# Reciprocal root of a variance: two ScalarE activations and one Newton step in place of a bit trick with longer refinement

## The chip, the core and the metric

The kernel runs on one core of a Trainium2 chip. A core has five engines with an instruction queue each, which run in order and meet only at semaphores: TensorE (PE in the profile), VectorE (DVE), ScalarE (ACT), GpSimd (POOL) and SyncE (SP, which only issues transfers here). The metric is the device time of one execution in microseconds (us), the median of several runs. Lower is better.

## What is computed

Eight blocks (the batch), each of 4096 positions with 32 channels, pass through a linear-attention layer and then through a mixture of 8 experts. Three normalisations over the 32 channels of a position lie on the way; each needs one over the square root of a variance for each position:

```python
def _ln_c(v, eps=1e-06):                       # LN1, input of the attention
    m = jnp.mean(v, axis=1, keepdims=True)
    s = jnp.var(v, axis=1, keepdims=True)
    return (v - m) / jnp.sqrt(s + eps)
...
out = (out - mean) * jax.lax.rsqrt(var + LN_EPS) * g_ln[None, :, None, None]   # LN2, end of the attention
...
def _ln_t(v, eps=1e-05):                       # LN3, input of router and experts
    return (v - m) / jnp.sqrt(s + eps)
x = x + _L0_conv_ref(_ln_c(x), ...)
t = t + _L0_ffn_ref(_ln_t(t), ...)
```

The attention takes a softmax of queries and keys; the second part picks the two best of eight experts for each position and adds their outputs with gates.

## The kernel before

**Tiling.** A block is held as 128 partitions by 32 groups of positions, so that a statistic of a normalisation is a tile of 128x32 numbers (`vsum`, `vari`, `root`, `rr`, `ru`, `rstd`, one of each for LN1, LN2 and LN3), while the data is 128x1024.

**Order.** The order on each engine is written out by hand. The function `iteration(i, cur, prev, nxt, ahead)` goes through 26 steps, and tables with names AT_... say which unit of work stands in which step. An iteration works on four blocks at once: the last part (experts) of block i-1 (`prev`), the attention, LN2 and LN3 of block i (`cur`), the keys and queries of block i+1 (`nxt`), and the load and LN1 of block i+2 (`ahead`). It runs for i = -2 to 8: at -2 only `ahead`, at -1 `nxt` and `ahead`, at 0 all but `prev`, from 1 to 5 all four, at 6 no `ahead`, at 7 only `cur` and `prev`, at 8 only `prev`.

**One normalisation.** DVE sums (`mean`), POOL subtracts the mean (`centered`, L417), ACT squares (`squares`, L486), DVE sums the squares (`vsum`, L653) and then makes the reciprocal root in `inverse_root` (L647): `vari` (L656), a first guess from the bits of the number (`root`, L658), and seven further small steps up to `rstd` (L661 to L679). Each of them waits for the one before. Then POOL multiplies by `rstd` (L422 for LN1 and LN3, L463 for LN2). For LN1 and LN3 ACT then rounds the result twice into `parts` (`high_parts`, L495 and L496), DVE makes the remainder (`low_part`, L684), and TensorE turns the `parts` around through `narrow` (`make_stack`, L842), from where ACT copies them (L490).

**Where the three stand.** LN2: `AT_RSTD2` = steps 10, 11, 11, 12. LN3: `AT_RSTD3` = 19, 19, 20, 20. LN1: `AT_RSTD1` = 22, 23, 23, 24, with LN3's `low_part` (step 22) between the sum and `vari`.

**The turn of an iteration.** TensorE writes `query_logits` of units 0 and 1 (step 0) into the two slots of `narrow`; ACT takes the exponential of each (`query_exp`, tile `eq`, L510), which frees the slot; only then can `make_stack` of LN3's data (step 1) write there. On ACT the two `high_parts` of LN3 (step 22) stand just ahead of these exponentials. On DVE stand at that place: the end of LN3, `sums_ctx` (L733), `grec` (L736), `mix` (L738), `mixz` (L742), `vsum` of LN1, `low_part` of LN3, and the whole root of LN1. TensorE's small product between `sums_ctx` and `grec` is `mix_context` (step 22). `ws_kmax` (L727, step 12) is the DVE addition before which no key logits can be made.

**Tables.** ACT's functions read a table set that an ACT_TABLE_LOAD brings in; before, there is one, ahead of the first copy.

Of the kernel before, what the change touches and what calls it, by code (L numbers as in the profile page):

```python
# [33 lines left out]
P = 128  # L34
G = N // P
# [19 lines left out]
AT_X2 = 13  # L55
AT_CENTER3 = 15
AT_SCALE3 = 21
AT_RSTD2 = (10, 11, 11, 12)
AT_MEAN3 = 15
AT_SQUARE3 = 18  # L60
AT_RSTD3 = (19, 19, 20, 20)
AT_SPLIT3 = 22

AT_STACK3 = (1, 1, 2, 3)
# [9 lines left out]
AT_MEAN1 = 20  # L74
AT_CENTER1 = 20
AT_SQUARE1 = 21
AT_RSTD1 = (22, 23, 23, 24)

AT_SCALE1 = 2
AT_SPLIT1 = 3  # L80
# [16 lines left out]
def build(nc, x, w_qkv, b_qkv, w_out, b_out, g_ln, router_w, router_b, expert_w, expert_b, out):  # L97
# [6 lines left out]
    with ctx:  # L104
# [54 lines left out]
        vsum = {k: sb(f"vsum{k}", [P, G]) for k in LN}  # L159
        vari = {k: sb(f"vari{k}", [P, G]) for k in LN}  # L160
        root = {k: sb(f"root{k}", [P, G]) for k in LN}
        rr = {k: sb(f"rr{k}", [P, G]) for k in LN}
        ru = {k: sb(f"ru{k}", [P, G]) for k in LN}
        rstd = {k: sb(f"rstd{k}", [P, G]) for k in LN}
# [60 lines left out]
        center_ready = {k: sem(f"center_ready{k}") for k in LN}  # L225
        square_ready = {k: sem(f"square_ready{k}") for k in LN}
        rstd_ready = {k: sem(f"rstd_ready{k}") for k in LN}
        xhat_ready = {k: sem(f"xhat_ready{k}") for k in (1, 3)}
        high_ready = {k: sem(f"high_ready{k}") for k in (1, 3)}
        parts_ready = {k: sem(f"parts_ready{k}") for k in (1, 3)}  # L230
# [13 lines left out]
        norm_v = sem("normalise_vector_steps")  # L244
        ln23_v, route_v = sem("layernorm23_vector_steps"), sem("route_vector_steps")
        heads_p, ln2_p, gates_p = sem("heads_pool_steps"), sem("layernorm2_pool_steps"), sem("gates_pool_steps")
        LN1_V, KQ_V, LN23_V, ROUTE_V = 10, 5, 19, 14

        class Chain:

# [227 lines left out]

        @block.scalar
        def _(act):  # L480
            def set_up():
                act.wait_ge(setup_v, SETUP_V)

            def square(k, b):
                act.wait_ge(center_ready[k], 4 * b + 4 if k == 2 else b + 1)
                nc.scalar.activation(squares[k][:], centered[k][:], ACT.Square).then_inc(square_ready[k], 1)  # L486

            def copy_stack(k, pos, u):
                act.wait_ge(narrow_full, pos.n + pos.stack[k][u] + 1)
# [29 lines left out]
            def iteration(i, cur, prev, nxt, ahead):  # L519
                f, g, n, m, pos = i, i - 1, i + 1, i + 2, Places(i, cur, prev, nxt, ahead)  # L520
                for step in STEPS:
                    for u in units(ahead, AT_XT, step):
                        act.wait_ge(narrow_full, pos.n + pos.xt[u] + 1)
                        if cur and u == 0:
                            act.wait_ge(x2_ready, f + 1)
                        nc.scalar.copy(x_tok[:, m % 2, 512 * u:512 * u + 512],
                                       narrow[:, pos.xt[u] % 2, :]).then_inc(narrow_free, 1)
                    for u in units(prev, AT_STACK3, step):
                        copy_stack(3, pos, u)
                    for u in units(cur, AT_QEXP, step):  # L530
                        query_exp(pos, f, u)
                    if ahead and step == AT_SQUARE1:
                        square(1, m)
                    if prev and step == AT_ROUTER:
                        act.wait_ge(small_full, pos.s + pos.logit + 1)
                        nc.scalar.copy(logit[:].rearrange("p g e -> p (g e)"),
                                       small[:, 0:G * E]).then_inc(small_free, 1)
                    if prev and step == AT_RESIDUAL:
                        act.wait_ge(x2_ready, g + 1)
                        if not (isinstance(g, int) and g == 0):  # L540
                            act.wait_ge(out_full, OUTU * g)
                        nc.scalar.copy(residual[:], x2[:]).then_inc(residual_ready, 1)
                    if prev and step == AT_E2:
                        act.wait_ge(gap_ready, g + 1)
                        nc.scalar.activation(e2[:], gap[:], ACT.Exp, scale=wscale[:, 2:3]).then_inc(e2_ready, 1)
                    if nxt and step == AT_SPLIT1:
                        high_parts(1, n, xhat[:, :, 0:C])
                    for u in units(nxt, AT_STACK1, step):
                        copy_stack(1, pos, u)
                    if cur and step == AT_SQUARE2:  # L550
                        square(2, f)
                    if cur and step == AT_SQUARE3:
                        square(3, f)
                    for u in units(nxt, AT_KEXP, step):
                        key_exp(pos, n, u)
                    for half in units(nxt, AT_QROWS, step):
                        act.wait_ge(narrow_full, pos.n + pos.qrows[half] + 1)
                        nc.scalar.copy(qmax_tr[:, half, :],
                                       narrow[:, pos.qrows[half] % 2, 0:P // 2].bitcast(f16)).then_inc(narrow_free, 1)
                    if prev and step in AT_OUT[3::4]:  # L560
                        copy_output(g, AT_OUT.index(step) // 4)
                    if cur and step == AT_SPLIT3:
                        high_parts(3, f, xhat3[:])
# [5 lines left out]
        def _(dve):  # L569
# [77 lines left out]
            def inverse_root(k, c, b, eps, part):  # L647
# [6 lines left out]
                elif part == 1:  # L654
                    c.wait()
                    c.inc(nc.vector.tensor_scalar(vari[k][:], vsum[k][:], 1.0 / C, eps, ALU.mult, ALU.add))  # L656
                    c.wait()
                    c.inc(nc.vector.tensor_scalar(root[k][:].bitcast(i32), vari[k][:].bitcast(i32), -0.5,  # L658
                                                  float(0x5F1FFFF9), ALU.mult, ALU.add))
                    c.wait()  # L660
                    c.inc(nc.vector.tensor_tensor(rr[k][:], root[k][:], root[k][:], ALU.mult))  # L661
                elif part == 2:
                    c.wait()
                    c.inc(nc.vector.scalar_tensor_tensor(ru[k][:], rr[k][:], -0.375 * 0.703952253, vari[k][:],
                                                         ALU.mult, ALU.mult))
                    c.wait()
                    c.inc(nc.vector.scalar_tensor_tensor(root[k][:], ru[k][:], 0.375 * 0.703952253 * 2.38924456,
                                                         root[k][:], ALU.add, ALU.mult))
                    c.wait()
                    c.inc(nc.vector.tensor_tensor(rr[k][:], root[k][:], root[k][:], ALU.mult))  # L670
                else:
                    c.wait()
                    c.inc(nc.vector.scalar_tensor_tensor(ru[k][:], rr[k][:], 64.0 / 9.0, vari[k][:],
                                                         ALU.mult, ALU.mult))
                    c.wait()
                    c.inc(nc.vector.scalar_tensor_tensor(rr[k][:], ru[k][:], -10.0 / 3.0, ru[k][:],
                                                         ALU.add, ALU.mult))
                    c.wait()
                    nc.vector.scalar_tensor_tensor(rstd[k][:], rr[k][:], 5.0, root[k][:], ALU.add,  # L679
                                                   ALU.mult).then_inc(rstd_ready[k], 1)  # L680

            def low_part(k, b, src):
# [358 lines left out]
```

## Time and profile of the kernel before

| | us |
|---|---|
| median of 3 runs | 584.05 (583.22 to 585.13) |
| the profiled execution | 585.64 |
| its span in the trace | 583.9 |

| engine | busy us | share of the span |
|---|---|---|
| PE | 413.1 | 71% |
| DVE | 412.1 | 71% |
| ACT | 236.5 | 41% |
| POOL | 218.9 | 37% |

No engine is busy throughout. So the table alone doesn't say what bounds the kernel; for that one reads the chain that ended last (each piece of work followed back to what released it) and, at a place of interest, the timelines of all engines side by side. In a row of a timeline the first number is the start in us from the start of the span, the second the busy time, and the bracket at the end, where there is one, the idle time before it and what ended it.

### The profile page before, as it was taken

What the parts mean: (1) busy time and instruction counts of PE and PEld (TensorE: products, weight loads), DVE (VectorE), ACT (ScalarE), POOL (GpSimd) and SP (SyncE); (2) the same over time, 40 slices, a digit from 0 to 9 for tenths busy, and PEclk for the clock granted to TensorE, in tenths of its full rate; (3) what the DMA queues carried; (4) which work ended last, traced back from release to release, by engine and by line L of the source; (5) the groups of instructions that cost most, each with busy time, mean ns of one, the idle gap of its engine ahead of it and who ended that gap; (6) DMA issues with size and microseconds to landing.
All of it is one profiled execution on the core that took longest, in us unless ns stands there. A gap on an engine that the chain in (4) does not pass through costs nothing.

```text
span 583.9 us, 9061 instructions
## 1 busy us (share of the span) xinstructions
PE 413.1 (71%) x3632; PEld 329.4 (56%) x3632; DVE 412.1 (71%) x803; ACT 236.5 (41%) x321; POOL 218.9 (37%) x192
## 2 busy tenths in 40 slices
PE   1149968767978497948985797949795898365371
PEld 1027746655767286827764486828682776254261
DVE  0655788599768987598759975898769863864540
ACT  1044635660467035731475046712582137103200
POOL 8200663372336342552237223634255221741100
PEclk9998989795989699877989697959988898885586
DMA  2100000000011000100010001100000001000001
GB/s 50 36 1 1 37 1 12 26 1 2 1 31 43 1 1 12 63 1 1 2 43 30 1 1 35 40 0 1 12 27 2 1 0 38 0 2 16 20 1 36
DMA packets 4257, 9.17 MB, mean 16 GB/s; under 512 B 2134, under 2 KB 2168, under 8 KB 4216
## 3 DMA queue, kind: packets, MB, share of 16 engines
q1 hardware_dynamic: 4216, 8.59, 4.8%
q8 instruction: 29, 0.48, 0.3%
q14 instruction: 12, 0.10, 0.1%
HBM read 4.40 MB, written 4.19 MB: 15 GB/s over the span
## 4 chain that ended last, share of the span: by engine, by line
PE 41%; DVE 36%; ACT 8%; issue 7%; POOL 5%; DMA 2%; POOLq 0%; PEldq 0%; DVEq 0%; ACTq 0%
PE wide L839 12%; PE sums L842 10%; PE small L839 8%; PE narrow L839 7%; DVE gated L785 5%; PE narrow L842 5%; DVE heads L705 5%; DVE kmax L713 4%; ACT stack L490 3%; POOL xhat L422 3%; DVE parts L684 2%; DVE vsum L653 2%; DVE tie L755 2%; DMA x_in<-in_x_dram 2%; DVE zrec L703 2%
## 5 line engine op out<-in xcount | busy, mean ns | idle before, releaser
L785 DVE TENSOR_TENSOR gated<-wide,gates 128x1024 f32<-128x1024 f32 x64 | 77.5, 1222 | 39.4 <-PE wide L839 36.1
L842 PE MATMUL sums<-ident,gated 128*128 128x128 f32 x512 | 79.4, 306 | 34.5 <-DVE gated L785 32.0
L502 ACT ACTIVATE ek<-narrow,wscale 128x512 f32<-128x512 f32 x64 | 44.0, 687 | 142.7 <-PE narrow L839 142.7
L842 PEld LDWEIGHTS sums<-ident,gated 128*128 128x128 f32 x512 | 65.5, 160 | 43.2 <-DVE gated L785 40.2
L839 PE MATMUL wide<-mixz,eq 128*128 128x132 f32 x512 | 73.5, 291 | 5.7 <-ACT stack L490 3.7
L490 ACT COPY stack<-narrow 128x1024 f16<-128x1024 f16 x64 | 63.0, 1014 | 35.1 <-PE narrow L842 35.1
L839 PE MATMUL wide<-w_stack,stack 128*128 128x128 f16 (+1 forms) x512 | 68.5, 280 | 6.9 <-DVE nqmax L690 2.7
L839 PEld LDWEIGHTS wide<-mixz,eq 128*128 128x128 f32 x512 | 65.0, 197 | 6.9 <-ACT stack L490 3.8
L839 PE MATMUL small<-ek,xhat 128*33 128x128 f32 x512 | 67.3, 278 | 0.0
L842 PE MATMUL narrow<-ident,parts 128*128 128x128 f16 x512 | 45.3, 250 | 28.9 <-ACT eq L510 18.9
L439 POOL TENSOR_TENSOR pairs<-heads 128x512 f32<-128x512 f32 x32 | 41.4, 1293 | 56.3 <-DVE heads L705 56.3
L842 PEld LDWEIGHTS narrow<-ident,parts 128*128 128x128 f16 x512 | 39.7, 114 | 33.8 <-DVE parts L684 23.7
L839 PEld LDWEIGHTS small<-ek,xhat 128*33 128x33 f32 x512 | 51.9, 111 | 9.1 <-issue 4.7
L839 PEld LDWEIGHTS wide<-w_stack,stack 128*128 128x128 f16 x512 | 44.3, 109 | 22.2 <-DVE kmax L713 10.0
L839 PE MATMUL wide<-stack,w_stack 128*128 128x512 f16 x64 | 25.1, 487 | 44.0 <-DVE kmax L713 33.3
L422 POOL TENSOR_TENSOR xhat<-centered,rstd 128x1024 f32<-128x1024 f32 x16 | 30.6, 1911 | 62.4 <-DVE rstd L679 62.4
L703 DVE RECIPROCAL zrec<-wide 128x16 f32<-128x16 f32 x64 | 16.4, 256 | 44.8 <-PE wide L839 44.1
L705 DVE TENSOR_TENSOR heads<-wide,zrec 128x512 f32<-128x512 f32 x64 | 44.3, 692 | 2.2
L510 ACT ACTIVATE eq<-narrow,wscale 128x512 f32<-128x512 f32 x64 | 43.1, 689 | 5.5 <-PE narrow L839 5.1
L690 DVE TENSOR_REDUCE nqmax<-wide 128x32 f32<-128x1024 f32 x32 | 39.0, 1219 | 8.6 <-PE wide L839 8.4
L417 POOL TENSOR_TENSOR centered<-x_tok,nmean 128x1024 f32<-128x1024 f32 x8 | 15.3, 1910 | 78.3 <-DVE nmean L645 78.3
L713 DVE TENSOR_REDUCE kmax<-wide 128x1 f32<-128x1024 f32 x32 | 38.1, 1220 | 5.2 <-PE wide L839 4.6
(138 smaller groups left out, 652.8 us busy)
## 6 DMA issues: line engine op xcount, KB each, us to landing
x_in<-in_x_dram SPq DMA_DIRECT2D x8, 512.0 KB
out_dram<-y_out SPq DMA_DIRECT2D x8, 512.0 KB
w_rows<-in_L_ffn_expert_w_dram SPq DMA_DIRECT2D x3, 32.0 KB
w_nat<-in_L_conv_w_qkv_dram SPq DMA_DIRECT2D x1, 48.0 KB
w_rows<-in_L_ffn_router_w_dram SPq DMA_DIRECT2D x3, 1.0 KB
w_rows<-in_L_ffn_expert_b_dram SPq DMA_DIRECT2D x2, 1.0 KB
w_rows<-in_L_ffn_router_b_dram SPq DMA_DIRECT2D x2, 0.0 KB
b_nat<-in_L_conv_b_qkv_dram SPq DMA_DIRECT2D x1, 1.5 KB
```

What stands on the lines that cost most here:

```text
L422: return nc.gpsimd.tensor_tensor(dst, tiles(centered[k][:]), per_tile(rstd[k]), ALU.mult)
L439: c.inc(nc.gpsimd.tensor_tensor(pairs[:, here, :], heads[:, here, 0:2 * C], heads[:, here, 2 * C:4 * C], ALU.add))
L490: nc.scalar.copy(stack[k][:, 1024 * u:1024 * u + 1024], narrow[:, pos.stack[k][u] % 2, :].bitcast(f16)).then_inc(narrow_free, 1)
L502: nc.scalar.activation(ek[:, u % EKS, :, :].rearrange("p a b -> p (a b)"), narrow[:, pos.kexp[u] % 2, :], ACT.Exp, scale=wscale[:, 0:1]).t ...
L510: nc.scalar.activation(eq[:, u % EQS, :], narrow[:, pos.qexp[u] % 2, :], ACT.Exp, scale=wscale[:, 0:1]).then_inc(narrow_free, 1)
L690: nc.vector.tensor_reduce(nqmax[:, half, 32 * (u % 2):32 * (u % 2) + 32], wide[:, pos.qmax[u] % 2, :].rearrange("p (a d) -> p a d", d=DH), ...
L703: c.inc(nc.vector.reciprocal(zrec[:, u % 2, :, :], src[:, :, P:P + HEADS]))
L705: nc.vector.tensor_tensor(heads[:, 4 * u:4 * u + 4, :].rearrange("p t (h c) -> p t h c", h=HEADS), src[:, :, 0:P].rearrange("p t (h c) -> ...
L713: nc.vector.tensor_reduce(kmax[:, u:u + 1], wide[:, pos.kmax[u] % 2, :], AX.X, ALU.max).then_inc(wide_free, 1)
L785: nc.vector.tensor_tensor(gated[:, u % GATEDS, :, :, :].rearrange("p e t c -> p t e c"), wide[:, pos.gate[u] % 2, :].rearrange("p (t e c) ...
L839: return nc.tensor.matmul(dst, lhs, rhs, start=start, stop=stop)
L842: return nc.tensor.matmul(dst, src, idt, is_transpose=True, start=start, stop=stop)
```

## The change

`inverse_root` now has three parts in place of four. DVE makes `vari` and tells ACT (`vari_ready`). ACT takes the logarithm of it (`lnvar`), waits for that on its own semaphore, and takes the exponential of -0.5 times it, which is `root` (`root_ready`). DVE waits for it and makes one Newton step in three instructions: `rr`, `ru`, `rstd`. For each of the 24 roots DVE has five instructions fewer (10 before, with `vsum`; 5 after), ACT two more. ACT's pair stands in step 11 for LN2 (`AT_ROOT2`), 20 for LN3 (`AT_ROOT3`) and 23 for LN1 (`AT_ROOT1`). ACT asks for the table set that has both functions at its start.

```diff
-AT_RSTD2 = (10, 11, 11, 12)
+AT_RSTD2 = (10, 11, 12)
+AT_ROOT2 = 11
...
-AT_RSTD3 = (19, 19, 20, 20)
+AT_RSTD3 = (19, 19, 20)
+AT_ROOT3 = 20
...
-AT_RSTD1 = (22, 23, 23, 24)
+AT_RSTD1 = (22, 23, 24)
+AT_ROOT1 = 23
...
+            nc.scalar.preload_act_table_set("natural_log_exp_and_others")
...
+            def first_root(k, b):
+                act.wait_ge(vari_ready[k], b + 1)
+                nc.scalar.activation(lnvar[k][:], vari[k][:], ACT.Ln).then_inc(lnvar_ready[k], 1)
+                act.wait_ge(lnvar_ready[k], b + 1)
+                nc.scalar.activation(root[k][:], lnvar[k][:], ACT.Exp, scale=-0.5).then_inc(root_ready[k], 1)
...
+                    if ahead and step == AT_ROOT1:
+                        first_root(1, m)
...
+                    if cur and step == AT_ROOT2:
+                        first_root(2, f)
...
+                    if cur and step == AT_ROOT3:
+                        first_root(3, f)
...
                     c.inc(nc.vector.tensor_scalar(vari[k][:], vsum[k][:], 1.0 / C, eps, ALU.mult, ALU.add))
                     c.wait()
-                    c.inc(nc.vector.tensor_scalar(root[k][:].bitcast(i32), vari[k][:].bitcast(i32), -0.5,
-                                                  float(0x5F1FFFF9), ALU.mult, ALU.add))
+                    dve.sem_inc(vari_ready[k], 1)
+                else:
+                    dve.wait_ge(root_ready[k], b + 1)
                     c.wait()
                     c.inc(nc.vector.tensor_tensor(rr[k][:], root[k][:], root[k][:], ALU.mult))
-                elif part == 2:
                     c.wait()
-                    c.inc(nc.vector.scalar_tensor_tensor(ru[k][:], rr[k][:], -0.375 * 0.703952253, vari[k][:],
-                                                         ALU.mult, ALU.mult))
+                    c.inc(nc.vector.scalar_tensor_tensor(ru[k][:], rr[k][:], -0.5, vari[k][:], ALU.mult, ALU.mult))
                     c.wait()
...
-                    nc.vector.scalar_tensor_tensor(rstd[k][:], rr[k][:], 5.0, root[k][:], ALU.add,
+                    nc.vector.scalar_tensor_tensor(rstd[k][:], ru[k][:], 1.5, root[k][:], ALU.add,
                                                    ALU.mult).then_inc(rstd_ready[k], 1)
```

What the change does to the order shows at the turn from iteration 1 to 2. On ACT, from LN1's square to the first exponentials of the next iteration, before (`parts` is LN3's, `eq` belongs to the next iteration):

```order
L486 ACTIVATE squares<-centered 128x1024
L517 COPY y_out<-sums 128x512
L495 CAST parts<-xhat 128x32x32
L496 CAST parts<-xhat 128x32x32
L510 ACTIVATE eq<-narrow,wscale 128x512 x2
```

On ACT at the same place, after (line numbers are those of the changed kernel; `lnvar` and `root` are the logarithm and the exponential of LN1):

```order
L495 ACTIVATE squares<-centered 128x1024
L532 COPY y_out<-sums 128x512
L510 CAST parts<-xhat 128x32x32
L511 CAST parts<-xhat 128x32x32
L499 ACTIVATE lnvar<-vari 128x32
L501 ACTIVATE root<-lnvar 128x32
L525 ACTIVATE eq<-narrow,wscale 128x512 x2
```

The pair stands between LN3's `parts` and the next iteration's `eq`. On DVE, from the end of LN3 to LN1's `vari`, before:

```order
L673 SCALAR_TENSOR_TENSOR ru<-rr,vari 128x32
L676 SCALAR_TENSOR_TENSOR rr<-ru 128x32
L679 SCALAR_TENSOR_TENSOR rstd<-rr,root 128x32
L733 COPY sums_ctx<-small 33x128
L736 RECIPROCAL grec<-small 128x1
L738 SCALAR_TENSOR_TENSOR mix<-small,grec,ctxscale 128x128
L742 TENSOR_TENSOR mixz<-mix,ctxbias 128x128
L653 TENSOR_REDUCE vsum<-squares 128x32
L684 TENSOR_TENSOR parts<-xhat,parts 128x32x32
L656 TENSOR_SCALAR vari<-vsum 128x32
```

On DVE after, from the end of LN3 through the whole root of LN1 to the first `zrec` of the next iteration:

```order
L683 TENSOR_TENSOR rr<-root 128x32
L685 SCALAR_TENSOR_TENSOR ru<-rr,vari 128x32
L687 SCALAR_TENSOR_TENSOR rstd<-ru,root 128x32
L741 COPY sums_ctx<-small 33x128
L744 RECIPROCAL grec<-small 128x1
L746 SCALAR_TENSOR_TENSOR mix<-small,grec,ctxscale 128x128
L750 TENSOR_TENSOR mixz<-mix,ctxbias 128x128
L674 TENSOR_REDUCE vsum<-squares 128x32
L692 TENSOR_TENSOR parts<-xhat,parts 128x32x32
L677 TENSOR_SCALAR vari<-vsum 128x32
L683 TENSOR_TENSOR rr<-root 128x32
L685 SCALAR_TENSOR_TENSOR ru<-rr,vari 128x32
```

LN1's `vari` has the same work in front of it as before, except for LN3's part, and its `rr` follows directly, with nothing between the two.

## Rows read from the trace of the kernel before

**Rows 1.** Page, part 1: busy time of an engine, share, instructions.

```profile
PE 413.1 (71%) x3632; PEld 329.4 (56%) x3632; DVE 412.1 (71%) x803; ACT 236.5 (41%) x321; POOL 218.9 (37%) x192
```

**Rows 2.** Chain in order of time, turn of iterations 3 to 4.

```profile
289.64 1.23 DVE gated L785
...
292.18 1.92 POOL xhat L422
...
295.07 1.04 ACT parts L496
```

**Rows 3.** Timeline of DVE, same turn.

```profile
292.01 0.28 DVE L733 COPY sums_ctx<-small 33x128 f32<-33x128 f32 x1
293.25 0.17 DVE L736 RECIPROCAL grec<-small 128x1 f32<-128x1 f32 x1 [0.96 <-PE small L839]
...
293.84 0.40 DVE L742 TENSOR_TENSOR mixz<-mix,ctxbias 128x128 f32<-128x128 f32 x1
...
295.29 1.21 DVE L684 TENSOR_TENSOR parts<-xhat,parts 128x1024 f16<-128x1024 f32 x1
296.42 0.17 DVE L656 TENSOR_SCALAR vari<-vsum 128x32 f32<-128x32 f32 x1
...
301.67 0.26 DVE L703 RECIPROCAL zrec<-wide 128x16 f32<-128x16 f32 x1 [3.28 <-PE wide L839]
```

**Rows 4.** Timeline of PE, same turn.

```profile
292.72 0.49 PE L839 MATMUL small<-u_mat,sums_ctx 33*128 33x129 f32 x2
...
296.84 1.80 PE L842 MATMUL narrow<-ident,parts 128*128 128x128 f16 x16 [2.65 <-ACT eq L510]
```

**Rows 5.** Timeline of ACT: first exponentials after three turns.

```profile
232.23 1.25 ACT L510 ACTIVATE eq<-narrow,wscale 128x512 f32<-128x512 f32 x2
...
296.02 1.26 ACT L510 ACTIVATE eq<-narrow,wscale 128x512 f32<-128x512 f32 x2
...
358.61 1.25 ACT L510 ACTIVATE eq<-narrow,wscale 128x512 f32<-128x512 f32 x2
```

**Rows 6.** Groups by line (instructions, busy us, mean ns, idle before): small ACT instructions.

```profile
L545 ACT ACTIVATE e<-gap,wscale 128x32 f32<-128x32 f32 x8 | 2.6, 321 | 21.7 <-DVE gap L766 21.7
...
L526 ACT ACT_TABLE_LOAD x1 | 1.3, 1283 | 0.8 <-PEq L1031 0.8
```

**Rows 7.** Timelines of ACT, DVE and PE, turn of iterations -1 to 0.

```profile
61.54 2.66 ACT L510 ACTIVATE eq<-narrow,wscale 128x512 f32<-128x512 f32 x4
...
61.58 0.29 DVE L742 TENSOR_TENSOR mixz<-mix,ctxbias 128x128 f32<-128x128 f32 x1
...
63.04 0.18 DVE L656 TENSOR_SCALAR vari<-vsum 128x32 f32<-128x32 f32 x1
...
62.28 0.39 PE L839 MATMUL narrow<-stack,w_stack 128*128 128x512 f16 x1 [0.34 <-ACT eq L510]
```

**Rows 8.** Timelines of DVE and PE, LN2 of block 0 and of block 3.

```profile
83.47 0.61 PE L839 MATMUL narrow<-ws_kmax,stack 128*128 128x128 f16 x4 [1.05 <-DVE ws_kmax L727]
...
268.68 1.22 DVE L785 TENSOR_TENSOR gated<-wide,gates 128x1024 f32<-128x1024 f32 x1 [0.33 <-PE wide L839]
```

**Rows 9.** Timelines of DVE and ACT: LN1 at the start; last output copy before LN3's parts.

```profile
18.61 0.18 DVE L656 TENSOR_SCALAR vari<-vsum 128x32 f32<-128x32 f32 x1
...
20.39 0.19 DVE L679 SCALAR_TENSOR_TENSOR rstd<-rr,root 128x32 f32<-128x32 f32 x1
...
534.03 0.58 ACT L517 COPY y_out<-sums 128x512 f32<-128x512 f32 x1 [7.75 <-PE sums L842]
535.01 1.04 ACT L495 CAST parts<-xhat 128x1024 f16<-128x1024 f32 x1 [0.39 <-POOL xhat L422]
```

**Rows 10.** Windows: stretch, its length, busy PE, PEld, DVE, ACT, POOL, PEclk, DMA, GB/s.

```profile
296.80:300.50 3.70, 3.41 (x26) 2.48 (x27) 1.35 (x8) 2.93 (x4) 1.91 (x1) 0.54 0.23 56
300.50:306.00 5.50, 5.50 (x75) 5.08 (x73) 2.48 (x6) 4.49 (x7) 1.35 (x2) 1.00 0.12 41
...
363.00:369.00 6.00, 6.00 (x56) 5.64 (x55) 1.90 (x4) 3.92 (x6) 0.73 (x2) 0.81 0.12 44
```

More of the change, by code:

```diff
@@ L161, in build @@
         root = {k: sb(f"root{k}", [P, G]) for k in LN}
+        lnvar = {k: sb(f"lnvar{k}", [P, G]) for k in LN}
         rr = {k: sb(f"rr{k}", [P, G]) for k in LN}
@@ L227, in build @@
         rstd_ready = {k: sem(f"rstd_ready{k}") for k in LN}
+        vari_ready = {k: sem(f"variance_ready{k}") for k in LN}
+        lnvar_ready = {k: sem(f"lnvar_ready{k}") for k in LN}
+        root_ready = {k: sem(f"root_ready{k}") for k in LN}
         xhat_ready = {k: sem(f"xhat_ready{k}") for k in (1, 3)}
@@ L246, in build @@
         heads_p, ln2_p, gates_p = sem("heads_pool_steps"), sem("layernorm2_pool_steps"), sem("gates_pool_steps")
-        LN1_V, KQ_V, LN23_V, ROUTE_V = 10, 5, 19, 14
+        LN1_V, KQ_V, LN23_V, ROUTE_V = 5, 5, 9, 14
         class Chain:
@@ L657, in inverse_root @@
                     c.wait()
-                    c.inc(nc.vector.tensor_scalar(root[k][:].bitcast(i32), vari[k][:].bitcast(i32), -0.5,
-                                                  float(0x5F1FFFF9), ALU.mult, ALU.add))
+                    dve.sem_inc(vari_ready[k], 1)
+                else:
+                    dve.wait_ge(root_ready[k], b + 1)
                     c.wait()
                     c.inc(nc.vector.tensor_tensor(rr[k][:], root[k][:], root[k][:], ALU.mult))
-                elif part == 2:
                     c.wait()
-                    c.inc(nc.vector.scalar_tensor_tensor(ru[k][:], rr[k][:], -0.375 * 0.703952253, vari[k][:],
-                                                         ALU.mult, ALU.mult))
+                    c.inc(nc.vector.scalar_tensor_tensor(ru[k][:], rr[k][:], -0.5, vari[k][:], ALU.mult, ALU.mult))
                     c.wait()
[L667 to L678, printed above, removed]
-                    nc.vector.scalar_tensor_tensor(rstd[k][:], rr[k][:], 5.0, root[k][:], ALU.add,
+                    nc.vector.scalar_tensor_tensor(rstd[k][:], ru[k][:], 1.5, root[k][:], ALU.add,
                                                    ALU.mult).then_inc(rstd_ready[k], 1)
```

## The prediction, made before the changed kernel had run

> **What bounds the kernel now.** I read the busy times first [rows 1]: PE and DVE are both at 71%, ACT at 41%. None of them is full, so a microsecond saved on DVE is worth something only where DVE's instruction is the late one. So the question is asked at each of the places where the root is computed: who is late there?
>
> The most telling place is the turn of an iteration, which the trace repeats almost to the hundredth from iteration 1 to 6. The chain goes [rows 2]: DVE's last gating of the iteration (289.64 to 290.87), LN3's last six small steps, POOL's scaling from 292.18, ACT's two castings into `parts`, and then the exponential `eq`, whose first starts at 296.02 [rows 5]. It frees the slot of `narrow` for which PE has sat idle for 2.65 us [rows 4]. So ACT's first `eq` is what all waits for at that turn. Beside this chain runs a second one on DVE. `grec` at 293.25 waits for PE's small product, which starts at 292.72 [rows 3, 4]. That product follows PE's own work without a gap: no idle time stands in its row, though `sums_ctx` was there at 292.29. After `grec` come `mix`, `mixz`, the sum of squares, `low_part` and at last `vari` of LN1, from 296.42 to 296.59 [rows 3]. That is 0.57 us **after** ACT has started `eq`. Before the change nobody on ACT needs this `vari`; and LN1's own result waits in turn behind other work on ACT.
>
> **The change part by part.**
>
> *Removed: five DVE steps for each of 24 roots.* A chained small step costs 0.22 us: from the start of `vari` at 18.61 to that of `rstd` at 20.39 are eight steps [rows 9]. That is 24 x 5 x 0.22 = 27 us of DVE time, of which only what lies on a late path counts.
>
> *Added on ACT: the pair.* The trace has no logarithm and no exponential with a constant scale on such a tile. Nearest is the exponential of the gates, 0.321 us for the same 128x32 shape with a scale read from memory [rows 6]: high end. Low end is DVE's step on the same tile, 0.17 us [rows 3]. I take 0.27 each, nearer to ACT's own row. The hand-over from DVE to ACT, with its separate semaphore step, I take at 0.08. Its low end is 0.04, what lies between two chained steps of DVE (0.22 less 0.18 [rows 9]); its high end is 0.14, from the end of the first `eq` (296.02 and half of 1.26 + 0.09) to PE's start at 296.84 [rows 4, 5]. Between logarithm and exponential stand 0.04, and an instruction that waits for nothing starts 0.09 before the one ahead ends (`parts` ends at 296.11, `eq` starts at 296.02 [rows 2, 5]). Together, from the end of `vari` to the start of the next ACT instruction: 0.08 + 0.27 + 0.04 + 0.27 - 0.09 = 0.57 us (0.33 to 0.73). The Trainium skill, in "ScalarE: Activation LUTs", section "What ACT_TABLE_LOAD costs", puts an ACTIVATE with constant operands at 186 ns and 0.833 ns for each element, 213 ns here; by that page, an estimate, each turn would be 0.11 us cheaper and the whole 0.8 us faster.
>
> *The turn, iterations 1 to 5.* In ACT's queue the pair of LN1 stands between LN3's `parts` and `eq`. LN3's end is shorter by three steps (0.67 us), so ACT is through with `parts` at 295.4 in place of 296.11 [rows 2]. There it must wait, and behind it are queued both `eq`, which have their inputs, and behind those PE's `make_stack`. What it waits for doesn't come earlier: `vari` hangs on `grec` and PE's product, which didn't wait for DVE. Only `mixz` helps a little: it took 0.40 beside the end of POOL's scaling [rows 3] and 0.29 where POOL was idle [rows 7], 0.11 less. So `eq` starts at 296.59 - 0.11 + 0.57 = 297.05 in place of 296.02: +1.0 us a turn (bounds 0.8 to 1.3, the latter without the help), and the 0.67 us of LN3 are lost in the wait. Five turns: **+5.0**.
>
> *The turn from 0 to 1.* There PE's product did wait for `sums_ctx`, which stands behind LN3. The second chain moves forward by 0.67 too: **+0.3**.
>
> *The turn from -1 to 0.* No LN3 yet, and `eq` starts early, at 61.54, while `vari` ends at 63.22 [rows 7]. Now `eq` starts at 63.22 + 0.57 = 63.79: **+2.2**. PE's next query logits at 62.28 waited for exactly this `eq` [rows 7], so nothing hides it.
>
> *LN2.* Around step 11 ACT has nothing to do until PE's key logits, so the pair costs it nothing. DVE loses five steps in step 11, but the gating behind them waits for PE anyway (0.33 us idle, 268.68 [rows 8]), and the last part has three steps as before. **0** from iteration 1 on; the cover is PE's work, and without it up to -1.1 a block would come. In iteration 0 no gating stands there: `ws_kmax` came behind the root, and PE waited 1.05 us for it [rows 8]. Its input is there 0.7 us earlier than it was used: **-0.7**.
>
> *LN3 where no LN1 follows.* Iteration 6: three steps less on the chain, **-0.7**. Iteration 7: ACT's output copy ends at 534.61, and `parts` started at 535.01 [rows 9], so only **-0.4**. At steps 19 and 20 themselves LN3's pair is made while ACT has time, long before DVE needs it.
>
> *LN1 of block 0.* Alone on the chip: from `vari` on 8 steps of 0.22 before; now hand-over and pair (0.08 + 0.27 + 0.04 + 0.27 + 0.08 = 0.74) and 3 steps, against the 8 of before: 1.78 - 0.74 - 0.67 = **-0.4** (-0.6 to -0.2).
>
> *TensorE's clock.* After the 2.65 us of idle PE runs at a mean granted clock of 0.54 of full speed, which is almost all the time at 1.2 GHz, for 3.7 us; then it is back at 1.00, or one turn later in part only (0.81) [rows 10]. At the turn from -1 to 0 PE had no such gap; now it has one of 2.6 us. Half speed over 3.6 us costs at most 1.8 us; some of it lies beside ACT's work: **+1.2** (0 to 1.8). The Trainium skill, "TensorE: Matmul & The Clock Gate", section "HAM oscillation — how this bites in real kernels", names the same mechanism: waits inside a loop bring the slow clock back each time. The trace agrees at every turn; it shows no gap of this length at -1 to 0, where the rule would add this term.
>
> Sum: 5.0 + 0.3 + 2.2 - 0.7 - 0.7 - 0.4 - 0.4 + 1.2 = **+6.5 us**. The profiled execution took 585.64 (583.9 of span and 1.7 around it) and would take 592.1. The median of the runs lies 1.6 below it; so the forecast is 584.05 + 6.5 = **590.5 us**.
>
> **The rivals.**
>
> *A. The delay is swallowed and the savings stay: 581.7.* Behind the turn lies a stretch in which DVE works almost without a pause (heads and routing). If that stretch already had its start from DVE's own work, a late `eq` would be hidden up to the slack, and what counts would be -0.4 - 0.7 - 0.7 - 0.4 = -2.2. It decides if DVE's first `heads` doesn't move against the last gating. Against it: DVE idles for 3.3 us before its first `heads` after the turn, waiting for PE [rows 3], and the chain runs from `eq` over PE and ACT into the stretch. 0.08.
>
> *B. Within a measurement of the old time: 584.3.* The periods between turns alternate: 63.79 us from 232.23 to 296.02, 62.59 from there to 358.61 [rows 5], three long and two short in five. The difference follows the clock after the gap [rows 10]: back at 300.5 in one, slow for some 2.3 us longer in the other. If the shifted turns all fall on the good side, three long ones give back 3.6 us, and with the low end of the pair (-1.4 for seven turns) and no clock loss at the first turn (-1.2) it is 590.5 - 6.2 = 584.3. 0.08.
>
> *C. All on the bad side: 595.* The same alternation the other way: +2.4 for the two short ones, and the high ends of the pair, +2.0 for seven turns: 594.9. 0.05.
>
> *D. The pair changes tables.* If logarithm and exponential, or the copies around them, lay in different sets, two loads of 1.28 us [rows 6] would stand in each pair, seven of them in front of `eq`: +18 or more, 608. The changed program has one load in ACT's queue, as before. "ScalarE: Activation LUTs" of the Trainium skill, section "Table sets: the hidden batching unit", also has both functions in one set. 0.02.
>
> **How the numbers follow.** The forecast has 0.77. About 0.3% (1.75 us) is what a measurement of this kernel can tell from no change. Faster: A, 0.08. Same: B, 0.08. Slower: the forecast, C and D, 0.84. The range runs from 585.8, which leaves out A and B, to 594.5, which leaves out the most of C and D; inside lie the pair's bounds (-1.4 to +2.0) and about two thirds of the alternation of the clock.
>
> **What would show it.** In the profile of the changed kernel ACT should wait for DVE's `vari` after LN3's `parts` at seven turns, by about 0.9 us from iteration 1 on, with `eq` about 0.5 us behind the end of `vari`, and PE's idle time before `make_stack` should grow from 2.65 to about 3.7 us. DVE's busy time should fall by about 23 us, to 389, and ACT's rise by 13, with the period still growing. The forecast is wrong if `vari` of LN1 comes much earlier against the last gating, if the idle time before `make_stack` doesn't grow, or if the clock after the turns settles on one side.

## The result, and the profile after

The changed kernel takes **593.12 us** (median of 4 runs, 593.05 to 594.4) against 583.63 of the kernel before on the same chip (4 runs, 581.54 to 585.13): a ratio of **1.017, 95% interval 1.0135 to 1.0205**. It is slower by 9.5 us where +6.5 was forecast, inside the range. The profiled execution of after took 593.05 with a span of 591.3; that of before was one of its longer ones (585.64, span 583.9), so the two traces differ by 7.4 us only, and the other 2 us lie in the choice of the execution. One execution each of e9, e11 and e12 ran slow throughout (granted clock 0.71 to 0.78) and is left out of all times and ratios.

The page of after, busy time by engine (against [rows 1]):

```profile
PE 413.7 (70%) x3632; PEld 331.7 (56%) x3632; DVE 390.1 (66%) x683; ACT 246.5 (42%) x369; POOL 219.1 (37%) x192
```

DVE has lost 22.0 us of work in 120 instructions, ACT has got 10.0, and the span has grown. The groups by line of after (instructions, busy us, mean ns | idle before and its releaser) show the pair, DVE's first step behind it, and the one table load (against [rows 6]):

```profile
L499 ACT ACTIVATE lnvar<-vari 128x32 f32<-128x32 f32 x24 | 5.4, 227 | 74.1 <-DVEq L679 74.1
L501 ACT ACTIVATE root<-lnvar 128x32 f32<-128x32 f32 x24 | 5.5, 229 | 0.8
L683 DVE TENSOR_TENSOR rr<-root 128x32 f32<-128x32 f32 x24 | 4.5, 186 | 5.1 <-ACT root L501 5.1
L488 ACT ACT_TABLE_LOAD x1 | 1.3, 1283 | 0.8 <-PEq L1039 0.8
```

Logarithm and exponential take 0.23 us each, where 0.27 was taken. That is nearer to the 0.213 (an estimate) that follows from the formula of the Trainium skill ("ScalarE: Activation LUTs", section "What ACT_TABLE_LOAD costs"). One table load stands there as before.

At the turn from iteration 3 to 4 the timeline of ACT in after (start, us, what, idle before) reads:

```profile
298.58 1.04 ACT L511 CAST parts<-xhat 128x1024 f16<-128x1024 f32 x1
300.76 0.23 ACT L499 ACTIVATE lnvar<-vari 128x32 f32<-128x32 f32 x1 [1.14 <-DVEq L679]
301.02 0.23 ACT L501 ACTIVATE root<-lnvar 128x32 f32<-128x32 f32 x1
301.16 1.25 ACT L525 ACTIVATE eq<-narrow,wscale 128x512 f32<-128x512 f32 x2
```

The timeline of DVE at that turn (against [rows 3]):

```profile
293.83 1.23 DVE L793 TENSOR_TENSOR gated<-wide,gates 128x1024 f32<-128x1024 f32 x1 [1.25 <-PE wide L847]
...
297.43 0.17 DVE L744 RECIPROCAL grec<-small 128x1 f32<-128x1 f32 x1 [1.37 <-PE small L847]
...
298.02 0.29 DVE L750 TENSOR_TENSOR mixz<-mix,ctxbias 128x128 f32<-128x128 f32 x1
...
299.36 1.22 DVE L692 TENSOR_TENSOR parts<-xhat,parts 128x1024 f16<-128x1024 f32 x1
300.49 0.18 DVE L677 TENSOR_SCALAR vari<-vsum 128x32 f32<-128x32 f32 x1
301.28 0.19 DVE L683 TENSOR_TENSOR rr<-root 128x32 f32<-128x32 f32 x1 [0.61 <-ACT root L501]
...
307.94 0.26 DVE L711 RECIPROCAL zrec<-wide 128x16 f32<-128x16 f32 x1 [6.01 <-PE wide L847]
```

And PE's product for `grec`, and its make_stack behind the turn (against [rows 4]):

```profile
296.91 0.49 PE L847 MATMUL small<-u_mat,sums_ctx 33*128 33x129 f32 x2
...
301.97 1.87 PE L850 MATMUL narrow<-ident,parts 128*128 128x128 f16 x16 [3.59 <-ACT eq L525]
```

Read it from PE upwards. PE idles 3.59 us in place of 2.65 (this idle time ahead of make_stack is called the gap from here on), until `eq` frees `narrow`. `eq` starts when the pair is through. The pair waits 1.14 us with ACT idle, because `vari` ends at 300.67, and `grec` in front of it still waits for PE, now 1.37 us in place of 0.96: what LN3 saves is lost there. DVE's own idle time before the first `zrec` grows from 3.28 to 6.01 us.

The turns side by side, in us. "Gated to eq" runs from the start of the last gating to that of the first `eq`; "eq to heads" from there to the start of the last `heads` behind it (`heads` is what DVE makes of PE's products with `eq`, eight times in a block); "rest" is what is left of the period up to the next turn's `eq`.

```
turn                     -1>0   0>1    1>2    2>3    3>4    4>5    5>6    6>7
first eq, before        61.54 105.71 169.62 232.23 296.02 358.61 422.35 483.79
first eq, after         63.45 108.46 172.27 236.57 301.16 365.87 430.66 492.72
difference               1.91   2.75   2.65   4.34   5.14   7.26   8.31   8.93
gated to eq, before                    6.37   6.37   6.37   6.37   6.37   6.37
gated to eq, after                     7.33   7.33   7.33   7.33   7.33   5.69
eq to heads, before     13.63  21.18  19.91  21.09  19.91  21.04  19.91  19.84
eq to heads, after      15.24  20.16  20.65  20.92  21.06  21.12  21.15  20.59
rest, before            30.54  42.73  42.70  42.70  42.68  42.70  41.53
rest, after             29.77  43.65  43.65  43.67  43.65  43.67  40.91
```

Two things stand in it. The rest of the period grows by 0.95 us and is otherwise constant: this is the plain delay. What alternated in before lies wholly between `eq` and the last `heads`, and it goes with TensorE's clock. Before, the slow level lasts 6.8 us at one turn and 3.4 us at the next; after, it lasts 6.8 us at each turn from 0>1 to 5>6. At 6>7 it is 3.4 us in both. The windows of after, from the gap to where the clock is back (columns as in [rows 10]; the clock is the last but two):

```profile
297.50:301.90 4.40, 0.88 (x10) 0.53 (x8) 3.65 (x9) 3.20 (x7) 0.10 (x1) 0.90 0.19 39
301.90:307.80 5.90, 5.58 (x35) 4.59 (x36) 0.03 (x1) 3.80 (x5) 1.91 (x1) 0.50 0.18 60
307.80:312.00 4.20, 4.20 (x52) 3.79 (x51) 2.20 (x6) 3.35 (x5) 1.14 (x1) 1.00 0.18 59
```

All of PE's work in the 5.9 us behind the gap is done at 0.50 of full speed, 1.2 GHz; in before it was 3.7 us at 0.54 in this very turn. One turn later, from 4 to 5, before has its long stretch:

```profile
358.50:365.30 6.80, 5.61 (x36) 4.62 (x37) 2.21 (x10) 4.67 (x7) 1.91 (x1) 0.51 0.22 66
```

### The profile page after: what moved, and what is told of

The parts are those of the page before. It is cut to its first block, busy times and chain, and to the rows that moved or that the text cites. A ratio compares the mean times of both kernels' runs of the same rounds, so it can differ in the third digit from the quotient of the medians.

```text
span 591.3 us, 9037 instructions
## 1 busy us (share of the span) xinstructions
PE 413.7 (70%) x3632; PEld 331.7 (56%) x3632; DVE 390.1 (66%) x683; ACT 246.5 (42%) x369; POOL 219.1 (37%) x192
## 4 chain that ended last, share of the span: by engine, by line
PE 43%; DVE 36%; ACT 8%; issue 7%; POOL 2%; DMA 2%; POOLq 0%; DVEq 0%; PEldq 0%; ACTq 0%
PE wide L847 12%; PE sums L850 11%; PE small L847 10%; PE narrow L847 6%; DVE heads L713 4%; PE narrow L850 4%; DVE kmax L721 4%; ACT stack L505 3%; DVE vsum L674 3%; DVE gated L793 3%; DVE parts L692 3%; DMA x_in<-in_x_dram 2%; DVE nqmax L698 2%; DVE tie L763 2%; DVE zrec L711 2%
## 5 line engine op out<-in xcount | busy, mean ns | idle before, releaser
L847 PE MATMUL wide<-mixz,eq 128*128 128x132 f32 x512 | 77.2, 301 | 5.6 <-ACT stack L505 3.7
L847 PEld LDWEIGHTS wide<-mixz,eq 128*128 128x128 f32 x512 | 68.7, 206 | 6.8 <-issue 3.2
```

Of the source, the lines that this page charges most:

```text
L847: return nc.tensor.matmul(dst, lhs, rhs, start=start, stop=stop)
```

## The experiments

Three theories went in. **Theory 1, the place**: ACT's queue works in order, the pair stands in front of `eq`, and the wait for LN1's `vari` is what costs. **Theory 2, the clock**: the wait is only the trigger, and a good part of the time is the slow clock after a longer gap. **Theory 3, the pair itself**: the two instructions and the hand-overs between engines cost, wherever they stand.

**e1: the pair of LN1 behind the first `eq`.** The changed kernel with one thing moved, block 0 apart:

```diff
+                    if nxt and step == 0 and not (isinstance(n, int) and n == 0):
+                        first_root(1, n)
...
-                    if ahead and step == AT_ROOT1:
+                    if ahead and step == AT_ROOT1 and isinstance(m, int) and m == 0:
                         first_root(1, m)
```

> The changed kernel with one edit: ACT makes LN1's logarithm and exponential behind the next iteration's first two exponentials eq instead of in front of them (block 0 excepted). Theory 1 (the wait and the pair in front of eq delay TensorE at seven turns): PE's idle time before make_stack falls from 3.59 to 2.5 us or less, each turn gives back about 1.0 to 1.1 us and the first one 1.9; 593.1 - 5 x 1.05 - 1.9 - 0.9 and some clock = 583 or less, and with the savings of the other places (ws_kmax, LN3's end) about 581. Theory 2 (the loss is mostly TensorE's clock, that recovers later since the changed order happens to fall badly): the gap still exceeds 2.4 us, so the clock still drops, and the time stays above 587. Theory 3 (two more ACT instructions for each root and their hand-overs cost wherever they stand): about 590.

Measured: 578.34 us, ratio 0.990 (0.987 to 0.992), some 3 us below what theory 1 said. The same instructions in another place turn a loss of 1.7% into a gain of 1.0%. ACT's timeline of e1 at the turn from 3 to 4:

```profile
290.50 1.04 ACT L511 CAST parts<-xhat 128x1024 f16<-128x1024 f32 x1
291.45 1.26 ACT L525 ACTIVATE eq<-narrow,wscale 128x512 f32<-128x512 f32 x2
292.68 0.23 ACT L499 ACTIVATE lnvar<-vari 128x32 f32<-128x32 f32 x1
```

PE's timeline of e1 there:

```profile
292.56 1.34 PE L852 MATMUL narrow<-ident,parts 128*128 128x128 f16 x16 [2.25 <-DVE parts L694]
```

`eq` follows `parts` at once, and "gated to eq" is 5.70, which is the 6.37 of before less LN3's three steps (0.67). But PE's idle time is shorter by 0.40 only: the releaser is no longer `eq` but DVE's low part, which in before had ended at 296.50, 0.34 us ahead of make_stack. Theory 3 falls: the pair is in all 24 places here, and the kernel is faster than before.

**e2: the wait alone.** The kernel before, where ACT waits for LN1's `vari` at step 23 and does nothing with it; all nine steps stay on DVE:

```diff
+                    if ahead and step == 23:
+                        act.wait_ge(vari_ready, m + 1)
...
+                    if k == 1:
+                        dve.sem_inc(vari_ready, 1)
```

> The kernel before with nothing but a wait added: ACT waits for DVE's variance of LN1 between LN3's castings and the next eq; no logarithm, no exponential, all DVE steps as before. Theory 1: the wait alone costs 0.57 + 0.1 us at each of six turns and 1.7 + 0.1 at the first: +5.8 us, 589.5, and PE's idle time before make_stack grows from 2.65 to about 3.3 us. Theory 3 (the ACT instructions are the cost): no more than +1 us, 584.5. Theory 2: between them, with the periods between turns at 64 us or more even so.

Measured: 595.18 us, ratio 1.019 (1.016 to 1.023). No arithmetic is moved, and the kernel is slower by 11.8 us. ACT at the turn from 3 to 4 of e2:

```profile
299.67 1.04 ACT L497 CAST parts<-xhat 128x1024 f16<-128x1024 f32 x1
301.28 1.26 ACT L511 ACTIVATE eq<-narrow,wscale 128x512 f32<-128x512 f32 x2 [0.57 <-DVEq L662]
```

The wait moves `eq` by 0.67 us at five turns (gated to eq 7.04), by 1.8 at the first and 0.46 at 0>1 (rest 31.00 for 30.54), 5.6 us together. That is what theory 1 had (5.8), and so is PE's gap of 3.32 us; but its time was 589.5. The rest lies in the stretch behind the gap: "eq to heads" is 20.76, 21.11, 21.28, 21.34, 21.36 and 21.38 from turn 0>1 on, 4.2 us more than the six of before. What is left to 11.8 is about what the profiled execution of before lies over its median. The windows of e2:

```profile
301.90:307.90 6.00, 5.54 (x35) 4.54 (x36) 1.03 (x6) 3.94 (x6) 1.91 (x1) 0.50 0.20 61
```

So theory 2 holds as an amplifier: with a wait of 0.57 us in front of the gap the slow stretch is the long one at each turn from 0>1 to 5>6.

**e3 and e4: one half of the change each.** In e3 LN1 alone uses ACT, in e4 LN2 and LN3 alone; what is left has the nine steps and their old places in the order:

```diff
+                (root_by_act if k in (1,) else root_by_bits)(k, c, b, eps, part)
```

(in e4 `k in (2, 3)`).

> Only LN1's root by ACT, LN2 and LN3 as before. Theory 1: all of the loss and none of the gains of the other two: DVE's chain to LN1's variance unchanged, turns +1.05 (without the help to mixz) x 6, first turn +1.9, start -0.4: +8 to +10 us, 592 to 594. Theory 3: a third of the whole, +3, 587.

> Only LN2's and LN3's roots by ACT, LN1 as before (nine DVE steps). Theory 1: faster than before: -0.7 at ws_kmax of block 0, up to -0.2 at each turn (PE is then held by low_part on DVE, which ends 0.2 us before the old release), -0.7 and -0.4 at the last two LN3: -2 to -3 us, 581 to 582. Theory 3 (each pair costs): slower than before, 586 to 588.

Measured: e3 594.0 us, ratio 1.017 (1.014 to 1.021), gated to eq 7.43, PE idle 3.70 before make_stack. e4 580.63 us, ratio 0.994 (0.991 to 0.996), gated to eq 5.70, PE idle 2.25 and released by DVE's low part. Both came as theory 1 said. LN1's place carries the whole loss. For LN2 and LN3 the change pays, 2.8 us. The halves make 7.8 (+10.6 and -2.8) where the whole is 9.5; each of the three has an interval of 1.5 to 2 us to either side, so these times don't settle whether the halves add.

**e7: LN1's variance earlier.** The changed kernel with `AT_RSTD1 = (22, 22, 24)`, so that `vari` stands ahead of the low part in DVE's queue:

> The changed kernel with DVE making LN1's variance ahead of LN3's low_part (AT_RSTD1 22, 22, 24): ACT's wait for it all but vanishes at six turns, its pair still stands in front of eq. Theory 1: eq starts about 1.1 us earlier against the last gating at five turns, low_part 0.2 us later; the first turn is unchanged: 593.1 - 5 to 6 = 587.5. Theory 3 (the pair itself is the cost): no change, 592 to 593.

Measured: 584.61 us, ratio 1.001 (0.999 to 1.003), no difference from before. ACT's timeline of e7 at the turn from 3 to 4:

```profile
295.59 1.04 ACT L511 CAST parts<-xhat 128x1024 f16<-128x1024 f32 x1
296.76 0.23 ACT L499 ACTIVATE lnvar<-vari 128x32 f32<-128x32 f32 x1
297.02 0.23 ACT L501 ACTIVATE root<-lnvar 128x32 f32<-128x32 f32 x1
297.15 1.25 ACT L525 ACTIVATE eq<-narrow,wscale 128x512 f32<-128x512 f32 x2
```

PE's timeline of e7 there:

```profile
298.09 1.89 PE L850 MATMUL narrow<-ident,parts 128*128 128x128 f16 x16 [2.71 <-DVE parts L692]
```

ACT no longer waits to speak of; 0.13 us lie between `parts` and the logarithm. "Gated to eq" is 6.32, against 5.70 in e1 and 7.33 in after: the pair in front of `eq` delays it by 0.62 us, and the wait for `vari` by another 1.01. LN3's 0.67 pays for the pair. But the low part is late instead, and PE idles 2.71 us for it, 0.06 more than before. "eq to heads" alternates again between about 21.2 and 20.0, as in before (1.4 us less than after over the six turns), and its first turn has no slow stretch (1.6 us less, see below); theory 1 had 587.5. At the turns from 1>2 on it is the wait that made the kernel slower than before, not the pair.

**e5, e6 and e8: PE kept busy in the gap.** Sixteen matmuls of 128x128 in fp32 ahead of make_stack, into a part of `small` that nobody reads, put into before (e5), after (e6) and e1 (e8), at every turn but the first:

```diff
+                    if cur and prev and step == 1:
+                        pe.wait_ge(small_free, pos.s)
+                        for _ in range(16):
+                            mm(small[:, 384:512], ident[:], ones[:])
```

> The kernel before with 16 extra matmuls (their result is never read) on TensorE in its gap of 2.65 us before make_stack, at the seven turns that have an earlier block (iterations 1 to 7); they take 1.7 to 1.9 us at full clock. It measures what the clock costs at a turn. Theory 2 (the clock after the gap is a large share of the difference): the granted clock after the gap stays at 1.00 and each of six turns gets 2 to 3 us shorter, 570 us or less. Theory 1 with a small clock share: the stretch behind the gap is paced by ACT and DVE as well, and at most 1 us a turn is gained, 577 or more; the alternation between periods of 62.6 and 63.8 us goes away in both.

> The changed kernel with the same 16 matmuls in the gap, which is 3.59 us here. If the clock is a large share of the 9.5 us between the two kernels, the difference between this and the filled kernel before shrinks to the plain delay of the turns: 6 x 0.95 + 1.9 - 1.5 = 6 us. If the clock has no share in it, the difference stays at 9 to 10 us.

> The changed kernel with LN1's pair behind eq and the 16 extra matmuls in TensorE's gap. If filling the gap pays, this is the fastest of all: below both kernels, by as much as the filled kernel before lies below the unfilled one. If the matmuls themselves run into the slow clock (16 of them then take 3.5 us), it is slower than the same without them.

Measured: e5 581.63 us, ratio 0.996 (0.994 to 0.998); e6 582.84, ratio 1.000 (0.997 to 1.003); e8 579.88, ratio 0.993 (0.990 to 0.996). PE's timeline of e5 at the turn from 3 to 4:

```profile
295.37 3.79 PE L839 MATMUL small<-ones,ident 128*128 128x128 f32 x32
298.99 1.06 PE L842 MATMUL narrow<-ident,parts 128*128 128x128 f16 x16
```

PE's timeline of e6 there:

```profile
293.89 3.79 PE L847 MATMUL small<-ones,ident 128*128 128x128 f32 x32
297.64 1.11 PE L850 MATMUL narrow<-ident,parts 128*128 128x128 f16 x16
```

Each of these matmuls shows as two records, and the filling lasts 3.8 us, twice what was expected. That is more than the gap in e5 and e8. There it pushes make_stack back and takes away what it brings: e5 gains 2 us where theory 2 said 13, and e8, expected to be the fastest, is no faster than e1. In e6 make_stack starts 0.81 us after `eq` (297.64 and 296.83), as in after (301.97 and 301.16). So e6 is the clean one up to the turn 5>6: nothing in after is faster or earlier, its work is only more, and it gains **10.3 us** on it (593.12 to 582.84; its ten executions lie between 579.9 and 587.1, and the interval of its ratio is 1.6 us to either side). At 6>7, where the gap of after is 1.97 us only, the filling is too long here too: "eq to heads" is 20.74 there. The windows of e6 behind the gap:

```profile
297.60:303.00 5.40, 4.50 (x52) 3.71 (x52) 0.95 (x2) 4.35 (x6) 1.91 (x1) 1.00 0.19 65
```

The clock stays at 1.00, make_stack takes 1.11 us in place of 1.87, and "eq to heads" is 19.30 at the turns 0>1 to 5>6. "Gated to eq" is still 7.33: the wait for `vari` is untouched.

**e9 to e12: a filling that fits, and the low part first.** e9 is e1 with 8 matmuls, e10 is before with 8. e11 is e1 with the pair one step later (`step == 1`) and `AT_RSTD1 = (23, 23, 24)`, so that the low part stands ahead of LN1's sum on DVE; e12 is e11 with 5.

> LN1's pair behind eq, and 8 extra matmuls in TensorE's gap in place of 16. With 16 the extra work lasted 3.6 us, longer than the gap of 2.26 us, and pushed make_stack back by some 1.3 us a turn; 8 last 1.9 us and fit. If the slow clock after the gap is what is left to gain, the clock stays at 1.00 and the time falls from 578.3 by 0.6 to 1.7 us a turn, to 571 to 574. If the clock drops in spite of it, 578.

> The kernel before with 8 extra matmuls in the gap of 2.65 us. They fit, so that the clock's whole share in the old kernel shows: the stretch from eq to the last heads falls from 19.9 and 21.1 us to 19.3 at six turns, -7 us, 577 (at least 580 if the clock still drops at some). Against it the filled changed kernel, 582.8, shows the plain delay of the changed order without the clock: theory 1 says 6 x 0.95 + 1.9 - 1.5 = 6 us between the two.

> LN1's pair behind the second two exponentials (end of step 1), and DVE makes LN3's low_part ahead of LN1's sum of squares. What released TensorE's make_stack in the kernel with the pair behind eq was low_part on DVE; it now comes 0.5 us earlier and eq is last again: 0.3 us a turn, 576 to 577. If DVE, held for the root ahead of the first heads, becomes the late one, 578 or more.

> The same with 5 extra matmuls (1.1 us) in the gap of about 2 us: if that is enough to keep the clock up, the fastest of all, 570 to 573; if not, as without them, 576 to 577.

Measured (medians):

```
                        us       ratio to before (95%)
e10 before, 8 filled    576.34   0.986 (0.984 to 0.989)
e9  e1, 8 filled        570.95   0.978 (0.975 to 0.980)
e11 low part first      579.02   0.990 (0.986 to 0.994)
e12 e11, 5 filled       570.98   0.978 (0.975 to 0.980)
```

PE's timeline of e10 at the turn from 3 to 4:

```profile
290.14 2.00 PE L839 MATMUL small<-ones,ident 128*128 128x128 f32 x16
292.96 1.11 PE L842 MATMUL narrow<-ident,parts 128*128 128x128 f16 x16 [0.81 <-ACT eq L510]
```

PE's timeline of e12 there:

```profile
288.38 1.33 PE L849 MATMUL small<-ones,ident 128*128 128x128 f32 x10
290.51 1.11 PE L852 MATMUL narrow<-ident,parts 128*128 128x128 f16 x16 [0.80 <-ACT eq L525]
```

Now the filling ends before `eq` frees the slot, 0.8 us of idle time are left, and the clock stays up: "eq to heads" is 19.31 at each turn of e10 from 0>1 to 5>6, and within 0.01 of that in e12 from 1>2 to 5>6. At 0>1 of e12, where 1.86 us are left idle behind the five matmuls, a slow stretch of 3.4 us follows (20.62). The kernel before gains 7.4 us by this alone. e12 and e9 are equal within their error, 2.2% faster than before, the best measured here and about where they were expected. e11 has three runs between 574.3 and 580.7 and can't be told from e1. Its profile shows PE idle 1.98 us, released by `eq` again, in place of 2.25: the low part is out of the way, but what that is worth in time stays open.

## Why the prediction was right, step by step

**The mechanism** was that of the trace: `vari` of LN1 ends after ACT would have started `eq`, ACT's queue holds `eq` behind the pair, and PE's make_stack waits. e2 shows it with the wait alone, e1 without it.

**The turns 1>2 to 5>6**: +1.0 each forecast, +0.95 measured (gated to eq 6.37 to 7.33), 4.8 for 5.0. From the end of `vari` (300.67) to `eq` (301.16) are 0.49 us where 0.57 were taken: 0.23 for 0.27 twice. `vari` itself starts 6.66 us after the last gating, 6.78 in before: the 0.11 of `mixz` (298.02, 0.29 us for 0.40), as worked out.

**The turn -1>0**: +2.2 and -0.4 for LN1 of block 0 make 1.8; the first `eq` is 1.91 later. That the sum fits so well is in part luck: executions whose instructions are the same up to there have it at 61.54 (before), 62.28 (e10) and 62.75 (e5), or at 63.45 (after, e7) and 61.99 (e6). The terms can be read without this scatter. `eq` started 1.68 us before the end of `vari` and now starts 0.49 behind it, 2.17 for 2.2. And block 0's `rstd` starts 1.25 us after its `vari` in place of 1.79, -0.54 for -0.4. ACT at that turn of after (against [rows 7]):

```profile
63.05 0.23 ACT L499 ACTIVATE lnvar<-vari 128x32 f32<-128x32 f32 x1 [1.91 <-DVEq L679]
...
63.45 2.64 ACT L525 ACTIVATE eq<-narrow,wscale 128x512 f32<-128x512 f32 x4
```

**LN2 of block 0, the turn 0>1**: -0.7 and +0.3 make -0.4; the rest of that iteration went from 30.54 to 29.77, -0.8. `ws_kmax` starts 8.03 us after the last `heads` in before and 7.22 in after, -0.81 for -0.7. From there to `eq` it is 22.51 and 22.55; but in e5 and e10, which are the kernel before up to there, it is 21.90 and 21.91. So the +0.3 lies between 0 and 0.65, within what executions differ by.

**LN2 from iteration 1 on**: 0 forecast; the rest of the period leaves no room for more than 0.01 besides the 0.95.

**LN3 of iteration 6**: -0.7 forecast, gated to eq 5.69 for 6.37, -0.68. But "eq to heads" behind it is 0.75 longer (20.59 for 19.84), a term that the prediction hadn't: the slow stretch lasts 3.4 us in both, and starts 2.8 us behind `eq` in place of 0.9. **LN3 of iteration 7**: -0.4 forecast. The last `rstd` starts 26.91 us after the last `heads` in after, e6 and e7, and 27.59 in e2, e5 and e10, whose LN3 is that of before: -0.68. ACT's output copy didn't stand in the way, since it moved too (ACT idles 0.70 us between it and `parts`). Whether the 0.68 reach the end of the kernel can't be read: the trace of before has PE at the slow level for 34 us near its end, that of after for 24.

**TensorE's clock was the term that was mis-sized.** The step says "**+1.2** (0 to 1.8)" for the first turn and takes the alternation of the others for something that stays as it is. At the first turn it was 1.6 us in the trace of after ("eq to heads" 13.63 to 15.24), with the gap of 2.49 us and the slow products behind it. PE there in after:

```profile
64.17 0.39 PE L847 MATMUL narrow<-stack,w_stack 128*128 128x512 f16 x1 [2.49 <-ACT eq L525]
...
65.20 1.81 PE L847 MATMUL wide<-mixz,eq 128*128 128x132 f32 x8
```

PE there in e7, which has the same gap at the same time:

```profile
64.18 0.39 PE L847 MATMUL narrow<-stack,w_stack 128*128 128x512 f16 x1 [2.49 <-ACT eq L525]
...
65.21 1.12 PE L847 MATMUL wide<-mixz,eq 128*128 128x132 f32 x8
```

In e7 the clock stays at 1.00 and "eq to heads" is 13.57. So the same gap costs 1.6 us in one execution and nothing in another, and the term is no fixed number.

At the other turns the alternation stopped on its bad side, as rival C had it, and cost 2.0 us over the six turns 0>1 to 5>6 in the traces. The fillings agree with that, but can't measure it. With the clock kept at 1.00 in both kernels at these turns, after and before stand at 582.84 (e6) and 576.34 (e10): +6.5 us, or 8.0 by their ratios. Without the filling it is 9.5, or 9.9 by the ratio. Each of these two differences has an interval of about 2 us to either side, so the difference of 1.9 to 3 us isn't clear of noise; and e6 has 16 matmuls to e10's 8, which cost it about 1.5 us at 6>7. What stands is the 2.0 us of the traces, at turns where the prediction had put the clock at nothing. One of the three signs that the prediction named for being wrong, the clock after the turns settling on one side, did come; the other two did not. The time still lies inside the range, 3 us above the forecast, because the range had left room for part of this. Rival C had the sign and the size of it, with a chance of 0.05: rows 5 and 10 had shown that the slow stretch has two lengths, and a gap longer by a third was a reason to expect the long one more often. Why it is the long one isn't shown. e7, with a gap of 2.71 us, still alternates, and e2 (3.32 us) and e3 (3.70 us) no longer do. But the length of the gap doesn't decide it alone: in e1 five turns in a row have 2.25 us, and one of them (2>3) has the long stretch, the other four the short one. Whether it is where in time the gap falls was not tested.

Rivals A and B are out by the measured ratio, and A by its own test: `heads` moved with `eq`, and later. D is out by the one table load. DVE's busy time (390.1 for 389) and ACT's (+10 for +13) came as worked out but for the shorter pair. ACT's wait was 1.14 us, where "about 0.9" was named as a sign; the prediction's own ends (295.4 for `parts`, 296.59 - 0.11 + 0.08 for the logarithm) give 1.16, so that figure was a slip, and no term hangs on it.

## What to carry to other kernels

Moving work to an engine that is 41% busy is free only where its queue has nothing behind it that is due before the work's input is there; look up what stands next in that queue and who waits for it, as with `eq` here: in front of it the pair cost 1.7%, behind it it gained 1.0%. Where TensorE idles for some us at every turn, measure the clock behind the gap before any trimming: five to eight matmuls that nobody reads gave 1.2 to 1.4% here, and the change itself 1.0% in its best place. And when a term alternates in the profile, forecast both of its sides: a small shift can settle it on one.

## Hardware behaviour that I had not expected

- The slow stretch behind a gap has two lengths here, 3.4 and 6.8 us. In before they take turns (gap 2.65 us), in after and e2 (gaps 3.59 and 3.32 us) it is the long one at each turn from 0>1 to 5>6. "Eq to heads" is 19.3 us with none; in before it is 19.9 with the short and 21.1 with the long one, in the other kernels, where the stretch begins earlier or later against `eq`, 19.8 to 20.7 and 20.2 to 21.6.
- The same gap doesn't always bring it: behind 2.49 us of idle PE at the first turn the products took 1.81 us in after and 1.12 in e7.
- So a wait is worth more than its length: 5.6 us of later `eq` cost 11.8 us in e2.
- Unused work on PE makes the kernel faster: -7.4 us in before (e10), -10.3 in after (e6), and it still pays when it leaves 0.8 us idle. Where it is longer than the gap it brings little (e5, -2) or nothing that can be told (e8 against e1).
- The hand-over between engines is small against the pair: 0.09 us from the end of `vari` (300.67) to the logarithm (300.76), and 0.03 from the end of `root` (301.25) to DVE's `rr` (301.28).
